# Shorter rows in the experts' table, a second small load for each tile, and fewer waits of GpSimd while it deals

## The reference, cut to what matters

```python
def _L1_ffn_ref(x, Wr, w1, w3, w2, s1, s3, s2):
    ...                                  # NUM_EXPERTS 8, TOP_K 2, n = 4096 tokens, h = 192, INNER = 768
    flat = x.reshape(n, h)
    probs = jax.nn.softmax(flat @ Wr, axis=-1)
    topk_p, topk_i = jax.lax.top_k(probs, TOP_K)
    topk_p = topk_p / jnp.clip(topk_p.sum(-1, keepdims=True), 1e-09)
    capacity = max(1, math.ceil(n * TOP_K / NUM_EXPERTS * CAPACITY_FACTOR))     # 1280
    ...
    order = jnp.argsort(-score, axis=1)[:, :capacity]
    ...
    dispatch = flat[order]
    gate = jax.nn.silu(jnp.einsum('ech,ehi->eci', dispatch, w1))
    up = jnp.einsum('ech,ehi->eci', dispatch, w3)
    expert_out = jnp.einsum('eci,eih->ech', gate * up, w2) * weight_sel[..., None]
    routed = jnp.zeros((n, h)).at[order.reshape(-1)].add(expert_out.reshape(-1, h))
    shared = jax.nn.silu(flat @ s1) * (flat @ s3) @ s2
    return (routed + shared).reshape(b, s, h)
```

## Time and profile before

| | |
|---|---|
| median of three runs | 2124.09 us |
| the profiled execution | 2119.34 us, of which the span of the profile is 2116.8 us |
| busy share: TensorE | 1894.8 us, 90% |
| VectorE | 1141.0 us, 54% |
| ScalarE | 738.8 us, 35% |
| GpSimd | 427.1 us, 20% |
| mean granted clock of TensorE | 0.942 |
| scatters `dealt<-e_x,slot` (L2450) | 64, 62.5 us busy, 139.6 us idle in front of them |
| loads of tiles `m_x<-dealt` | 40, 258.0 KB each |

### The profile page before, as it was taken

One profiled execution on the slowest core, in us unless ns is written; L12 is line 12 of the kernel. 1 busy time (PEld: TensorE's weight loads), 2 busy tenths in 40 slices (PEclk: granted clock), 3 DMA queues, 4 the chain that ended last, 5 costly groups with the idle time before them and its releaser, 6 DMA issues. The chain is left out here.

```text
span 2116.8 us, 28024 instructions
## 1 busy us (share of the span) xinstructions
PE 1894.8 (90%) x10067; PEld 1210.8 (57%) x10075; DVE 1141.0 (54%) x2777; ACT 738.8 (35%) x1248; POOL 427.1 (20%) x567
## 2 busy tenths in 40 slices
PE   4986558999999999779999997799969999999996
PEld 2343432454444444446666664465538888888886
DVE  5898668666666755368887774466211222222221
ACT  1434014455455545455555551221111211121111
POOL 5300210022012200111111120101551222322232
PEclk9988568999999999979999998899989999999998
DMA  2610021111111111000000000200213321222321
GB/s 64 223 52 0 1 71 62 51 38 62 44 46 53 53 53 31 24 10 10 6 6 6 6 6 0 101 1 13 72 55 91 71 61 33 62 59 65 69 37 20
DMA packets 68747, 94.73 MB, mean 45 GB/s; under 512 B 15386, under 2 KB 57662, under 8 KB 66337
## 3 DMA queue, kind: packets, MB, share of 16 engines
q1 hardware_dynamic: 52482, 77.19, 11.1%
q0 software_dynamic: 16128, 15.76, 4.2%
HBM read 54.96 MB, written 39.47 MB: 45 GB/s over the span
## 5 line engine op out<-in xcount | busy, mean ns | idle before, releaser
L1028 DVE TENSOR_REDUCE row_max<-c_ps_m 128x1 f32<-128x512 f32 x384 | 253.0, 687 | 112.3 <-PE c_ps_m L1198 106.8
L1376 ACT ACTIVATE e<-c_ps_s 128x512 f32<-128x512 f32 x384 | 216.5, 596 | 221.0 <-PE c_ps_s L1214 220.3
L2476 POOL DMA_INDIRECT out<-m_o,m_row_of x80 | 125.7, 1572 | 278.2 <-issue 250.2
L2675 DVE TENSOR_TENSOR e_f<-e_ps_u,e_gate 128x512 f32<-128x512 f32 x80 | 55.3, 692 | 205.5 <-PE e_ps_u L2866 205.5
L2936 ACT ACTIVATE e_gate<-e_ps_g 128x512 f32<-128x512 f32 x80 | 47.8, 597 | 334.2 <-PE e_ps_g L2866 334.2
L2876 PE MATMUL e_ps_o<-m_w,e_f 128*128 128x192 f32 x960 | 162.7, 326 | 0.9 <-DVE m_o L2683 0.9
L1198 PE MATMUL c_ps_m<-c_kT,qT 96*128 96x512 bf16 x384 | 150.0, 397 | 10.6 <-DVE row_max L1028 9.7
L1214 PE MATMUL c_ps_s<-qT,c_kT 97*128 97x512 bf16 x384 | 144.6, 386 | 13.0 <-ACT e L1376 5.6
L2876 PEld LDWEIGHTS e_ps_o<-m_w,e_f 128*128 128x128 f32 x960 | 155.1, 190 | 1.2 <-issue 1.2
L2683 DVE TENSOR_SCALAR m_o<-e_ps_o,m_w_of 128x192 f32<-128x192 f32 x80 | 29.7, 413 | 143.4 <-PE e_ps_o L2876 143.4
L1225 PE MATMUL c_ps_a<-e,v 128*32 128x512 f32 x768 | 105.5, 622 | 1.0 <-ACT e L1376 1.0
(11 more groups left out here) (469 smaller groups left out, 4071.9 us busy)
## 6 DMA issues: line engine op xcount, KB each, us to landing
dealt<-x SPq DMA_DIRECT2D x8, 1290.0 KB, 15.0
m_x<-dealt SPq DMA_DIRECT2D x40, 258.0 KB, 2.7
spread<-parts SPq DMA_DIRECT2D x24, 384.0 KB, 2.3
qT<-spread SPq DMA_DIRECT2D x144, 64.0 KB, 2.5
c_kT<-spread SPq DMA_DIRECT2D x144, 64.0 KB, 2.5
m_w<-in_w13e SPq DMA_DIRECT2D x8, 1152.0 KB, 5.1
m_w<-in_w2e SPq DMA_DIRECT2D x8, 576.0 KB, 6.2
out<-h SPq DMA_DIRECT2D x8, 384.0 KB, 4.5
```

What stands on the lines that cost most here:

```text
L1028: dve.tensor_reduce(row_max[:, n // J, n % J:n % J + 1], ps_m[:, n % 2, :], AX_X, ALU.max)\
L1376: act.activation(e[:, n % LIVE_E, :], ps_s[:, n % 2, :], ACT.Exp, scale=QSCALE).then_inc(e_ready, 1)
L2476: pool.indirect_dma_start(out=out_rows, out_offset=bass.IndirectOffsetOnAxis(ap=row_of[:, n % 2, r:r + 1], axis=0), in_=o[:, n % 2, r, :], ...
```

## The change

Rows of the experts' table become 194 numbers: weight, row number, and the 192 channels (TAGS = 2 stand in front, CD = 194). In `x1` and in the tile buffers a row keeps 258 numbers, the second copy now standing last. It is no longer dealt: a tile is loaded by two transfers, the first with the 194 numbers of each row, the second with channels 128 to 191 once more. Both count the same semaphore, and its readers wait for 32 in place of 16. The clearing of the table writes the shorter rows. In the dealing GpSimd waits for landings after each sixteenth transfer in place of each fourth. All column indices move accordingly.

```diff
-CX = CW + 2
+TAGS = 2
+CD = TAGS + C
+CX = TAGS + CW
...
-            sp.dma_start(xe[:, 0], dealt[0:CT, :].rearrange("(b p) c -> p b c", p=P)).then_inc(x_in[0], 16)
+
+            def load_rows(n):
+                rows = dealt[n * CT:(n + 1) * CT, :].rearrange("(b p) c -> p b c", p=P)
+                sp.dma_start(xe[:, n % 2, :, 0:CD], rows).then_inc(x_in[n % 2], 16)
+                sp.dma_start(xe[:, n % 2, :, CD:CX], rows[:, :, TAGS + P:CD]).then_inc(x_in[n % 2], 16)
+
+            load_rows(0)
...
-                sp.dma_start(xe[:, n % 2], dealt[n * CT:(n + 1) * CT, :].rearrange("(b p) c -> p b c", p=P))\
-                  .then_inc(x_in[n % 2], 16)
+                load_rows(n)
...
-                        in_=x1[:, b, :], in_offset=None, bounds_check=SLOTS - 1, oob_is_err=False
+                        in_=x1[:, b, 0:CD], in_offset=None, bounds_check=SLOTS - 1, oob_is_err=False
                     ).then_inc(scattered, 16)
-                    if (b + 1) % 4 == 0:
+                    if (b + 1) % 16 == 0:
                         pool.wait_ge(scattered, (k * NB + b + 1) * 16)
...
-                pool.wait_ge(x_in[n % 2], (n // 2 + 1) * 16)
+                pool.wait_ge(x_in[n % 2], (n // 2 + 1) * 32)
...
-                    pe.transpose(ps_te[:, 0, r * P:(r + 1) * P], xe[:, n % 2, r, 0:P], kit.ident[:, :])
-                    last = pe.transpose(ps_te[:, 1, r * P:(r + 1) * P], xe[:, n % 2, r, P:CW], kit.ident[:, :])
+                    pe.transpose(ps_te[:, 0, r * P:(r + 1) * P], xe[:, n % 2, r, TAGS:TAGS + P], kit.ident[:, :])
+                    last = pe.transpose(ps_te[:, 1, r * P:(r + 1) * P], xe[:, n % 2, r, TAGS + P:CX], kit.ident[:, :])
...
-    dealt = nc.dram_tensor("dealt", (SLOTS, CX), F32, kind="Internal").ap()
+    dealt = nc.dram_tensor("dealt", (SLOTS, CD), F32, kind="Internal").ap()
```

More of the change, by code:

```diff
@@ L240, in embed_and_route @@
         prob_rows = fresh[:, 0, 0:J * B * EXPERTS0].rearrange("p (j b e) -> p j b e", j=J, b=B)
-        zeros = x1[:, :, :].rearrange("p b c -> p (b c)")[:, NB * C - CAP * CX // P:]
+        zeros = x1[:, :, :].rearrange("p b c -> p (b c)")[:, NB * C - CAP * CD // P:]
         ps_rows = ps_o[:, :, :].rearrange("p a (b n) -> p (a b) n", b=2)
@@ L2431, in _ @@
             pool.wait_ge(made, 4)
-            pool.tensor_copy(x1[:, :, CW + 1], tag[:, :]).then_inc(made, 1)
+            pool.tensor_copy(x1[:, :, 1], tag[:, :]).then_inc(made, 1)
             root(6)
@@ L2444, in _ @@
                 if k == 1:
-                    pool.tensor_copy(x1[:, :, CW], weight[:, 1, :]).then_inc(w1_ready, 1)
+                    pool.tensor_copy(x1[:, :, 0], weight[:, 1, :]).then_inc(w1_ready, 1)
                     pool.wait_ge(w1_ready, 1)
@@ L2458, in meta @@
             def meta(n):
-                pool.wait_ge(x_in[n % 2], (n // 2 + 1) * 16)
+                pool.wait_ge(x_in[n % 2], (n // 2 + 1) * 32)
                 past(pool, oe_ready, n - 1)
-                pool.tensor_copy(w_of[:, n % 2, :], xe[:, n % 2, :, CW])
-                pool.tensor_scalar(row_of[:, n % 2, :], xe[:, n % 2, :, CW + 1], -1.0, float(N), ALU.mult, ALU.add)\
+                pool.tensor_copy(w_of[:, n % 2, :], xe[:, n % 2, :, 0])
+                pool.tensor_scalar(row_of[:, n % 2, :], xe[:, n % 2, :, 1], -1.0, float(N), ALU.mult, ALU.add)\
                     .then_inc(meta_ready, 1)
@@ L2492, in norm_apply @@
                 dve.wait_ge(rstd_ready, s + 1)
-                ln_apply(dve, x1[:, s * J:(s + 1) * J, 0:C], kit.h[:, s * J:(s + 1) * J, :], mv[:, s % 2],
+                ln_apply(dve, x1[:, s * J:(s + 1) * J, TAGS:CD], kit.h[:, s * J:(s + 1) * J, :], mv[:, s % 2],
                          rstd[:, s % 2]).then_inc(xn_ready, 1)
@@ L2572, in _ @@
             dve.tensor_tensor(rank8[:, :, :], hot[0][:, :, :], hot[1][:, :, :], ALU.add)
-            dve.tensor_copy(x1[:, :, CW], weight[:, 0, :])
+            dve.tensor_copy(x1[:, :, 0], weight[:, 0, :])
             hidden(9)
@@ L2700, in turned @@
                     b = s * J + half * 2 + r
-                    pe.transpose(ps_t[:, 0, r * P:(r + 1) * P], x1[:, b, 0:P], kit.ident[:, :])
-                    last = pe.transpose(ps_t[:, 1, r * P:(r + 1) * P], x1[:, b, P:CW], kit.ident[:, :])
+                    pe.transpose(ps_t[:, 0, r * P:(r + 1) * P], x1[:, b, TAGS:TAGS + P], kit.ident[:, :])
+                    last = pe.transpose(ps_t[:, 1, r * P:(r + 1) * P], x1[:, b, TAGS + P:CX], kit.ident[:, :])
                 last.then_inc(xT_psum, 1)
@@ L2900, in widened @@
                 act.wait_ge(xn_ready, s + 1)
-                act.activation(x1[:, blocks, C:CW], x1[:, blocks, P:C], ACT.Copy).then_inc(dup_ready, 1)
+                act.activation(x1[:, blocks, CD:CX], x1[:, blocks, TAGS + P:CD], ACT.Copy).then_inc(dup_ready, 1)
             def x_copy(s, half):
```

2 lines of the change are left out of this document (1 added, 1 removed).

## The result

The changed kernel is slower, not faster: 2153.32 us (median of four runs, 2149.93 to 2155.69) against 2125.09 (2122.7 to 2126.96) beside it, a ratio of 1.0134 with a 95% interval of 1.0120 to 1.0147. Its profiled span is 2151.0 us. The forecast of 2103.5 misses it by 50 us, far outside the range.

A forecast was written before the change was run, and what follows sets the result against it. GpSimd's dealing, stopping after every fourth scatter, kept TensorE idle 19.7 us before the first expert tile. Terms 19.83 + 0.83 - 0.1 = 20.6 us took the median 2124.09 to 2103.5 us, range 2101 to 2107, finally put at 2100.5 to 2108.

The forecast's parts named there:

- Waits of GpSimd: In the dealing, 12 waits for landings go and leave ordinary gaps; GpSimd is done 24.5 us sooner.
- What is late next: At the first expert tile, TensorE's last shared-expert pair, ending at 1568.98, and VectorE's product become late; 19.83 us gained.
- the cover of 4.4 us: The first expert tile's two loads are there by 1564.6, 4.4 us before TensorE asks.
- the 19.83 us: Gain from L2747's 48 matmuls beginning at 1569.81 instead of 1589.64.
- Idle time and clock: TensorE's 19.75 us idle before the first tile goes whole; 0.83 us more returns from the clock.
- the clock term: L2747's 48 matmuls take 8.07 us instead of 8.90 without an idle stretch ahead; 0.83 us gained.
- Shorter rows, second load, clearing: Scatters and table clearing gain nothing; the second load per tile costs 0.1 us in all, at a weight change.
- Rival 1: Second piece of a tile late at the six weight changes, costing up to 12 us: 2115.6 us; chance 0.07.
- Rival 3: GpSimd stalls in L2450 with sixteen transfers unfinished, slower than before from 1.36 us per scatter, 2162 us; chance 0.03.
- The signs that I named for "wrong": Scatters over 1.05 us, dealing waits much over 3, TensorE idle after weight loads, or waiting over 1 us for VectorE.
- the DMA share of 0.21: DMA share in 1486.9 to 1494, expected to reach 0.30 in the dealing, so no backlog at the remaining waits.
- eight gathers in a row: Evidence against slower transfers: the eighth of eight gathers without a wait took 0.94 us.

The follow-up runs named there:

- e2: The kernel before (rows of 258, one load per tile) with GpSimd waiting after every 16th scatter instead of every 4th; 2102.4 us, ratio 0.9899.
- e1: The changed kernel with the old waits, after every 4th scatter instead of every 16th; 2122.6 us, ratio 0.9997.
- e6: The kernel before (rows of 258) with GpSimd waiting for landings only after every 32nd scatter; 2170.5 us, ratio 1.0220.
- e8: The changed kernel with dealt rows of 226 numbers instead of 194, the second load bringing only the last 32 columns; 2143.6 us, ratio 1.0087.
- e9: The changed kernel plus a 64-number fill, not waited for, after each fourth scatter without a wait for landings; 2145.3 us, ratio 1.0107.
- e13: The changed kernel plus three 64-number fills, not waited for, after each fourth scatter without a wait for landings; 2129.3 us, ratio 1.0025.

## Why the prediction was wrong

**Waits of GpSimd: right.** 12 of them went, and the dealing shrank by 25.1 us (24.5 forecast).

**What is late next: this step failed.** It took the end of TensorE's last pair, 1568.98, over from the trace of before, as if nothing that GpSimd does could move it. In the changed kernel that pair ends at 1624.3, because TensorE does half its work while GpSimd scatters at 1.37 us each. Counted from the first scatter, it ends after 97.3 us in the kernel before and in e2, and after 148.6 us in the changed one. Everything behind this step, the cover of 4.4 us and the 19.83 us, was worked out from a number that the change itself moved. Against the forecast this is worth all of the 50 us: e2, whose TensorE isn't held up, has a span of 2100.7, the changed kernel one of 2151.0. By which path GpSimd's work holds up TensorE stays open.

**Idle time and clock: right, where TensorE isn't held up.** e2 gave 21.5 us for the forecast's 20.6. Its first tile is there at 1568.7, 4.5 us before TensorE asks for it (4.4 forecast), and its last 48 matmuls take the 8.07 us that the clock term counted on. In the changed kernel these parts bought nothing, since TensorE came to the first tile 51 us later than that.

**Shorter rows, second load, clearing: right.** e1 shows nothing for all of them together. The first load of a tile lands in 2.4 us, and TensorE has no wait for a tile in the expert stage of the changed kernel. Rival 1 didn't come: e1 has both loads at each of its 40 tiles, behind the weights too, and no wait of TensorE for a tile after the first (ratio 0.9997).

**The rivals.** Rival 3 had the right sign and the wrong engine: it looked for the price of many unfinished transfers in GpSimd's own scatters, with 1.36 us as its point of decision. They stayed at 0.974 us. The signs that I named for "wrong" were on GpSimd, its waits, the load and VectorE's last product, and none of them came. The row that was meant to speak against a backlog, the DMA share of 0.21, was read rightly and says nothing about TensorE. It was 0.18 in the stall, too. The other one, eight gathers in a row, ends where the trouble begins (by 1490, when the stall sets in, twelve scatters have begun): no row of before has more than eight scatters or gathers without a wait, and that lack should have widened the chance of "slower" far beyond 0.03.

## What to carry to other kernels

Waits of an engine can be a brake that protects others. When you remove them, ask which pace has never been seen in the trace, and take the numbers of the *other* engines in that stretch as unproven. Look at the busy time of all engines over the stretch and not only at the engine that was changed. And when a variant escapes a fault that its neighbours have, move it by a few us before you believe in what sets it apart: "short rows" outlived eleven kernels here and fell only to long rows in another layout and to a delay of 3 us.

## What the runs showed of the hardware

- Indirect scatters of GpSimd at a mean of 1.37 us each held up TensorE, and TensorE's counts of semaphores, late by 11.4 us (1488.6) and 20.6 us (1546.3), with DMA engines at a share of 0.18. The counts of VectorE and ScalarE that the trace has came within 0.1 us. In e2 the same pace held up nothing. By which path GpSimd's work reaches TensorE isn't shown.
- A late fetch of instructions looks like a consequence and not the cause. The page's queue "q8 instruction", which by its times brings TensorE's, fetches next in e2 at 1526.5 and in e6 at 1596.1, 50.5 and 119.2 us after the first scatter, but both times 0.4 us after the same matmul (L2722) had begun. So e6 lost its time over instructions for which e2 had no further fetch either. In e8 the fetch came 7 us after that spot, when the dealing was over.
- A wait of 3.7 us cost the 48 matmuls behind it 2.0 us (10.11 for 8.07), at a mean granted clock of 0.78; one of 19.7 us cost them 0.8.
- GpSimd's queue runs ahead of the engine: in the changed kernel it had done 16 of its `MOVE` instructions when 6 scatters had begun. In e6 it was never more than 13 ahead, and from then on went at the scatters' pace.
- Short fills behind a scatter cost next to nothing: one of 64 numbers disappears in the gap of 0.30 us between two scatters (e9), three add 0.2 us (e13).
